# A score's PSUM bank is chosen by a rule that counts banks read by VectorE as given back four turns later

## The reference

```python
x = L0(x)   # group norm, q k v, 8 heads of 32 channels: softmax(q k^T) v, projection, + x
x = L1(x)   # group norm, + pos; three small convolutions give spatial weights; group norm;
            # 8-head attention ("1") and two single-head attentions of 128 channels ("m");
            # concatenate, silu(ff1), ff2, out_w, group norm, + residual
x = L2(x)   # group norm, q k v, 8 heads of 32 channels, projection, + normed x
x = L3(x)   # group norm, q k v, one head of 256 channels, projection, + x

def attention(q, k, v):
    weight = jax.nn.softmax(einsum("bct,bcs->bts", q, k) * scale, axis=-1)
    return einsum("bts,bcs->bct", weight, v)
```

## Time and profile before

| | us |
|---|---|
| median of three runs | 5469.68 |
| lowest and highest run | 5468.94, 5470.98 |
| the profiled execution | 5462.21 |
| its span | 5460.3 |
| TensorE busy | 4989.7 |
| VectorE, ScalarE, GpSimd busy | 2960.1, 2558.3, 3239.2 |

### The profile page before, as it was taken

How to read it: one execution, slowest core, us unless ns; L and a number is a source line. 1 busy time by engine, 2 the same in 40 slices (tenths; PEclk the granted TensorE clock), 3 DMA queues, 4 the chain that set the end, 5 groups by cost and what they waited for, 6 DMA issues and landing times.

```text
span 5460.3 us, 63207 instructions
## 1 busy us (share of the span) xinstructions
PE 4989.7 (91%) x22016; PEld 2248.6 (41%) x22016; DVE 2960.1 (54%) x5256; ACT 2558.3 (47%) x4593; POOL 3239.2 (59%) x1777
## 2 busy tenths in 40 slices
PE   7789999999999999999999998999999999999887
PEld 3235333543335433354334543345333453334434
DVE  5445666256663566526665366634666346662362
ACT  3353545435553355524555245552555525454252
POOL 4474766546674477735767357654667636675463
PEclk8889989999899999999999999999999999899988
DMA  2112111022110211102210112101212012120020
GB/s 85 29 30 59 43 46 39 20 55 54 42 30 20 72 48 33 34 22 64 54 41 19 36 50 55 47 13 44 52 45 53 7 49 61 32 53 10 14 49 12
DMA packets 103608, 221.20 MB, mean 41 GB/s; under 512 B 31104, under 2 KB 33408, under 8 KB 103168
## 3 DMA queue, kind: packets, MB, share of 16 engines
q1 hardware_dynamic: 103296, 217.16, 15.5%
HBM read 56.47 MB, written 8.39 MB: 12 GB/s over the span
## 4 chain that ended last, share of the span: by engine, by line
PE 66%; DVE 11%; issue 9%; POOL 8%; ACT 4%; SPq 1%; DMA 1%; POOLq 0%; DVEq 0%; ACTq 0%
PE bank L518 66%; DVE max_cols L953 6%; POOL probs_added L1181 4%; POOL probs_added L1168 3%; ACT probs L854 2%; DVE act L1108 1%; ACT act L864 1%; DVE dev_squared L1071 1%; DVE stats L1057 1%; POOL act L1202 1%; SPq L1268 0%; DVE sums_turned L975 0%; SPq L1257 0%; DVE sums_turned L983 0%; ACT full_parts L919 0%
## 5 line engine op out<-in xcount | busy, mean ns | idle before, releaser
L953 DVE TENSOR_REDUCE max_cols<-bank 128x1 f32<-128x512 f32 x3456 | 2187.2, 679 | 1642.0 <-PE bank L518 1638.1
L854 ACT ACTIVATE probs<-bank 128x512 f32<-128x512 f32 x3456 | 1928.9, 599 | 2378.1 <-PE bank L518 2248.9
L1181 POOL TENSOR_TENSOR probs_added<-probs_added,probs 128x1024 f32<-128x1024 f32 x768 | 1807.6, 2382 | 131.8 <-ACT probs L854 131.3
L518 PE MATMUL bank<-q_stack,k_stack 97*128 97x512 f32 (+1 forms) x3584 | 1659.9, 520 | 147.2 <-DVE max_cols L953 107.8
L518 PE MATMUL bank<-probs,v_tokens 128*32 128x512 f32 (+1 forms) x7168 | 1392.8, 645 | 41.1 <-ACT probs L854 41.1
L518 PEld LDWEIGHTS bank<-q_stack,k_stack 97*128 97x128 f32 (+1 forms) x3584 | 661.5, 195 | 880.9 <-issue 429.5
L518 PE MATMUL bank<-act,weight_stream 128*128 128x512 f32 x1792 | 941.6, 625 | 31.6 <-ACT probs L854 8.0
L1181 POOL TENSOR_TENSOR probs_added<-probs 128x1024 f32<-128x1024 f32 x192 | 452.5, 2369 | 700.2 <-PE bank L518 673.0
L1168 POOL TENSOR_TENSOR probs_added<-probs 128x512 f32<-128x512 f32 x48 | 61.0, 1270 | 885.7 <-PE bank L518 853.3
L518 PEld LDWEIGHTS bank<-probs,v_tokens 128*32 128x32 f32 (+1 forms) x7168 | 329.6, 123 | 505.6 <-issue 350.8
L518 PE MATMUL bank<-high_parts 32*128 32x512 f32 x3072 | 406.1, 516 | 108.8 <-DVE max_cols L953 59.8
(11 more groups left out here) (84 smaller groups left out, 3390.4 us busy)
## 6 DMA issues: line engine op xcount, KB each, us to landing
k_stack<-high_parts SPq DMA_DIRECT2D x384, 128.0 KB, 2.4
q_stack<-high_parts SPq DMA_DIRECT2D x768, 64.0 KB, 2.0
weight_stream<-stream_dram SPq DMA_DIRECT2D x32, 768.0 KB, 4.3
k_stack<-low_parts SPq DMA_DIRECT2D x192, 128.0 KB, 2.4
q_stack<-low_parts SPq DMA_DIRECT2D x384, 64.0 KB, 2.0
act<-x_dram SPq DMA_DIRECT2D x8, 1024.0 KB, 6.5
act<-pos_dram SPq DMA_DIRECT2D x8, 1024.0 KB, 5.9
weight_stream<-stream_dram SPq DMA_DIRECT2D x16, 512.0 KB, 3.8
```

What stands on the lines that cost most here:

```text
L518: return nc.tensor.matmul(dst, lhsT, rhs, start=start, stop=stop, **kw)
L854: act.activation(PR[:, m % P_RING, j, :], bank[:, :], ACT.Exp, scale=att.scale).then_inc(reading(key), 1)
L953: dve.tensor_reduce(cols[:, kh, j, qt:qt + 1], bank[:, :], AX.X, ALU.max).then_inc(reading(key), 1)
L1181: pool.tensor_tensor(ADD[:, js, :], one, two, ALU.add).then_inc(p_added, 1)
```

## The change

Each bank gets a flag that says whether the tile last taken in it belongs to a kind that VectorE reads (maxima, columns, sums, value results, norm means and variances, projections, ff1). When a score tile takes its bank, the `given` turn of a flagged bank counts as four turns later. For all other tiles the choice is as before. The flag is set anew at each take. The plan, the instructions and their number stay as they are; which bank a tile sits in, and so which semaphore its first matmul waits for, changes.

```diff
+BY_VECTOR = ("max", "cols", "sums", "av", "av2", "mean", "var", "proj", "ff1")
+VECTOR_LATE = 4
...
             uses, fulls, given, held = [0] * BANKS, [0] * BANKS, [0] * BANKS, {}
+            by_vector = [False] * BANKS
 
             def take(key, hold=False, says_full=True):
 
-                bank = min((i for i in range(BANKS) if i not in held.values()), key=lambda i: (given[i], i))
+
+                late = VECTOR_LATE if key[0] == "score" else 0
+                bank = min((i for i in range(BANKS) if i not in held.values()),
+                           key=lambda i: (given[i] + late * by_vector[i], i))
+                by_vector[bank] = key[0] in BY_VECTOR
                 tiles[key] = bank, uses[bank], fulls[bank]
```

## The result

| | before | changed |
|---|---|---|
| median, us | 5469.31 (4 runs) | 5567.52 (4 runs) |
| profiled execution: span, us | 5460.3 | 5560.8 |
| its mean granted clock | 0.940 | 0.930 |

The changed kernel takes 1.0182 times as long as the one before, with a 95% interval of 1.0164 to 1.0199. The forecast was 5555 us, slower, within 5420 to 5640.

The account below looks back on a forecast made before the run. In-order TensorE, busy 91% of the span, bounds the kernel by its waits and clock. 5462.21 - 76 gained + 148 lost + 19 clock = 5553 us; with the median 7.5 above, 5561, rounded to 5555; range 5420 to 5640 us.

Parts of the forecast that it names:

- the three young prices: A score on the bank of the score one, two or three ahead loses 0.87, 0.57 or 0.27 us.
- the three quarters put down: Share of the summed stall losses expected to remain, a quarter being hidden as other engines catch up.
- 148 lost less 76 gained: Stall terms: 197 us lost less 49 hidden, against gains of 14 in kind 2 and 62 ahead of other scores.
- the change's 197 us: Loss before hiding: 103, 52 and 12 us on young banks, 22 behind q tiles, 8 in kind m.
- hardly anything is lost: Kind 0, score 50: its wait moves to an exponential already awaited by the value products; nothing of 23.2 us gained.
- the 8 us that I put down as lost: Kind m, score 9: its own matmuls, 1.1 us, move behind a wait for score 7's exponential, seven times.
- 2 us each, 14 of the 25.9 us: Kind 2, score 50: it goes some 3 us earlier, the quad behind it 2 us earlier, seven times.
- the three quarters of the rest: Of the remaining 82.5 us of VectorE-caused waits ahead of scores, 62 us gained; the rest met at quads.
- The clock: TensorE's half-speed time: 49 us more from added idle time, 30 us less from spared kind 2 stretches, net 19 lost.
- The first: Rival: long stalls behind VectorE decide, not short ones behind ScalarE; faster, 5375 us; chance 0.16.
- The second: Rival: waits only change their name, gain and loss cancel; 5470 us, 5459 to 5481 called same; chance 0.08.
- the third: Rival: stalls in a row lower the clock, no kind 2 stretches go, no losses hide; 5640 us; chance 0.14.

Follow-up runs that it names:

- e1: Changed kernel, but a score never takes the bank of a score one or two matmuls back: 5485.4 us, ratio 1.0042.
- e4: Kernel before, with every fourth score of kind 2 attentions forced onto the bank of the score directly ahead: 5521.9 us, ratio 1.0110.
- e8: Changed kernel, but a score never takes the bank of the score directly ahead; two ahead stays allowed: 5499.4 us, ratio 1.0061.
- e2: Changed kernel with VectorE's banks aged by one turn instead of four: 5457.3 us, ratio 0.9987.
- e3: Changed kernel with VectorE's banks aged by eight turns instead of four: 5878.6 us, ratio 1.0766.
- e5: Kernel before, with the four turns applied only to score 50 of the kind 2 attentions: 5460.6 us, ratio 0.9987.
- e10: Kernel before, no ageing, but a score never takes the bank of a score one or two matmuls back: 5459.5 us, ratio 0.9993.
- e6: Kernel before, each tile's bank from a list: the free bank read first in the trace of before: 5365.9 us, ratio 0.9810.

## Why the prediction was right, point by point

**What bounds.** TensorE, by its waits and its clock: the other engines' busy time hardly moved with the change (VectorE by 6.3 us, ScalarE by 10.7, GpSimd by 2.5) while the span grew by 100. The mechanism, young banks behind ScalarE, is shown by e1, e4 and e8.

**The price of a stall.** 1.17 us from start to start was forecast, 1.18 and 1.25 are in the rows. That is right. What is free between two scores was put at 0.3 us and is 0.34 in the trace, which makes the three young prices some 17 of 167 us too high. In e4 less of the price was kept than the three quarters put down: 55 us, or 59 us between the profiled spans, of 142.

**Two terms of the sum were probably too large, and they lie on opposite sides.** To see them apart I took the time from each matmul's start to the next one's in each trace, and from it the shortest usual time for the same pair of forms at the clock of that moment (the lowest tenth over all kernels). What is left over is stall; what the half clock adds to the shortest time is clock. Differences to the kernel before, in us:

| kernel | span | stall | clock |
|---|---|---|---|
| changed | +100 | +69 | +32 |
| e1, both young banks barred | +12 | +22 | -9 |
| e2, one turn | -14 | -10 | -4 |
| e3, eight turns | +417 | +307 | +110 |
| e4, pairs only | +59 | +76 | -17 |
| e5, score 50 only | -8 | +2 | -10 |
| e8, next one barred | +36 | +45 | -9 |
| e10, bar alone | -13 | -1 | -11 |

The split between the last two columns depends on what is called the shortest usual time: with the median in place of the lowest tenth the change reads +61 and +41, and e4 +82 and -23.

The forecast for the change was +72 stall (148 lost less 76 gained) and +19 clock. The difference of the two terms was right, and the difference is all that is measured. The terms themselves can only be estimated. The prices of e4 add up to 142 us and gave 76 of stall, so the share kept is 0.54 and not 0.75. With it the change's 197 us become 106, and only 37 us of gain are left where I had 76. From e1 (prices 161 x 0.27 + 22 + 8 = 73 us, stall +22) the two come out smaller still, a share of 0.4 and a gain of a few us. By these two kernels the gain was between some 5 and 40 us, and the loss between 75 and 106, and the two errors cancelled: that the forecast came so near is in part luck. The share is no constant, though. In e3 the prices come to 385 us, or 415 with q tiles and kind m, and the stall is +307, a share of 0.74 at least even if nothing was gained.

**Where a part of the loss went** can be seen in kinds 0 and m. In kind 0 the value products behind score 50 wait for a norm: its coefficients on VectorE (L1083, L1091 after), the apply and the exponential on ScalarE. Before (the rest is in the earlier trace rows), and then two samples of after:

```profile
589.12 2.29 DVE L1083 TENSOR_TENSOR gn_scale<-rstd,weights 128x2 f32<-128x2 f32 x1 [1.01 <-POOL rstd L1189]
```

```profile
587.07 2.31 DVE L1091 TENSOR_TENSOR gn_scale<-rstd,weights 128x2 f32<-128x2 f32 x1 [1.04 <-POOL rstd L1197]
...
591.85 0.80 PE L521 MATMUL bank<-q_stack,k_stack 97*128 97x512 f32 x1 [3.97 <-ACT probs L862]
...
592.57 1.94 PE L521 MATMUL bank<-probs,v_tokens 128*32 128x512 f32 x8
...
2611.09 2.31 DVE L1091 TENSOR_TENSOR gn_scale<-rstd,weights 128x2 f32<-128x2 f32 x1 [1.31 <-POOL rstd L1197]
...
2615.87 0.80 PE L521 MATMUL bank<-q_stack,k_stack 97*128 97x512 f32 x1 [1.32 <-ACT probs L862]
...
2616.59 1.94 PE L521 MATMUL bank<-probs,v_tokens 128*32 128x512 f32 x8
```

The value products start 4.76 us after the coefficients before, and 5.50 us after them in the changed kernel (5.20 in two of seven samples), however early or late TensorE comes there. The stall stayed, as forecast, and became a wait for ScalarE. But "hardly anything is lost" was not quite right: the score now stands behind the wait, and its own 0.7 us are lost each time (0.4 in two of seven samples). And the stall takes up what TensorE lost earlier: before it was 3.3 us in six of seven samples, now it is 3.97 or 3.98 in two and 1.32 to 1.48 in the other five, in which TensorE comes to score 50 some 3.3 us after the coefficients instead of at their start. Over the seven samples that is some 12 us that the changed kernel lost ahead of this place and that cost nothing.

In kind m the 8 us that I put down as lost were not lost. Right behind the maximum of the earlier trace rows (by the order of takes the first behind score 9, not the second) stands another wait, which I had not read:

```profile
1774.46 0.80 PE L518 MATMUL bank<-k_stack 128*128 128x512 f32 x1 [2.09 <-ACT probs L854]
```

This maximum waits for the exponential of score 8, and it starts 4.52 us after the norm's coefficients in both kernels. The score's matmuls that moved behind the first wait (4.19 us ahead of score 9 in the changed kernel) fit into the second one.


**Why the gain was small.** The step that failed is kind 2's stall ("2 us each, 14 of the 25.9 us"), and possibly with it the three quarters of the rest. In the changed kernel the same place reads:

```profile
751.00 0.50 PE L521 MATMUL bank<-q_stack,k_stack 97*128 97x512 f32 x1 [0.33 <-ACT probs L862]
...
752.14 0.50 PE L521 MATMUL bank<-q_stack,k_stack 97*128 97x512 f32 x1 [0.65 <-ACT act L882]
...
756.03 0.80 PE L521 MATMUL bank<-high_parts 32*128 32x512 f32 x4 [2.39 <-DVE max_cols L961]
...
755.81 2.79 DVE L1116 SCALAR_TENSOR_TENSOR act<-act 32x512 f32<-32x512 f32 x3
...
758.63 0.69 DVE L961 TENSOR_REDUCE max_cols<-bank 128x1 f32<-128x512 f32 x1
...
759.47 1.88 PE L521 MATMUL bank<-act,weights 96*32 96x512 f32 x2 [1.91 <-DVE max_cols L961]
```

Score 49 and the convolution in the timeline of before:

```profile
747.36 0.49 PE L518 MATMUL bank<-q_stack,k_stack 97*128 97x512 f32 x1 [0.34 <-ACT probs L854]
...
756.43 1.92 PE L518 MATMUL bank<-act,weights 96*32 96x512 f32 x2
```

The quad came earlier, as forecast: 5.03 us after the start of score 49 (751.00) instead of 6.78 (754.14 less 747.36), 1.75 us against my 2. What I had not done is read on. Score 51 was the next to wait for a maximum before, 0.76 us; now it doesn't, and the convolution behind it has got that maximum's bank. VectorE comes to this maximum only behind L1116 (L1108 before) and is done with it at 758.63 + 0.69 = 759.32. The convolution started 8.47 us after score 49 here and 9.07 before, so 0.60 us of the 1.75 are left; in e5, where score 51 waits for its maximum besides, it is 9.09 (754.38 less 745.29), and nothing is left. e5's ratio leaves 7 us of the 44 that I had put down there, clock and all.

**The quads.** I forecast their wait to stay near 109 us; it fell to 73.4, nearly all in the part that ScalarE causes. That fits: a score that has waited for an exponential leaves the quad less to wait for.

**The clock** was undersized, 19 against 32 us (41 by the other split). The mechanism, short stalls in a row, is seen at a place where the kernel before ran at full clock from 815 to 860 us. Stretches of before, then of after (columns as in the earlier trace rows):

```profile
815.00:860.00 45.00, 43.65 (x239) 18.71 (x231) 27.47 (x48) 27.44 (x52) 36.48 (x18) 1.00 0.17 41
```

```profile
827.00:836.00 9.00, 7.80 (x56) 2.32 (x48) 5.44 (x10) 4.14 (x9) 3.51 (x2) 1.00 0.34 82
836.00:846.00 10.00, 9.74 (x31) 2.89 (x31) 4.50 (x8) 3.31 (x6) 8.14 (x4) 0.50 0.01 2
...
863.00:870.00 7.00, 7.00 (x27) 2.60 (x30) 2.48 (x4) 3.19 (x7) 1.91 (x2) 0.53 0.37 83
```

The two matmul rows of after just ahead of the fall:

```profile
834.73 0.73 PE L521 MATMUL bank<-q_stack,k_stack 97*128 97x512 f32 x2 [0.69 <-ACT probs L862]
835.98 0.77 PE L521 MATMUL bank<-q_stack,k_stack 97*128 97x512 f32 x1 [0.51 <-ACT probs L862]
```

Stalls of 0.69 and 0.51 us, both on young banks, stand ahead of ten microseconds at half speed. The prediction had let the trace support what it names from the Trainium skill ("TensorE: Matmul & The Clock Gate", "A second HAM failure mode: psum-queue depth-cycling") for long stalls only; here it agrees for short ones. Even the trace of before has such falls, which the prediction had missed:

```profile
1553.48 0.50 PE L518 MATMUL bank<-q_stack,k_stack 97*128 97x512 f32 x1 [0.28 <-DVE max_cols L953]
```

```profile
1554.80:1568.40 13.60, 13.45 (x52) 4.48 (x44) 8.44 (x17) 7.06 (x13) 3.63 (x3) 0.50 0.12 29
```

Counted over the whole traces, 22 of 84 falls before, and 46 of 106 in the changed kernel, have no idle time of 1 us or more in the 8 us ahead (a choice of this count, not something the chip was seen to do). The half-speed time that starts so is 109 us before and 296 in the changed kernel, of 658 and 784 us in all. So the new half-speed time stands behind short stalls. But it isn't a rule of so much clock per stall: e4 has as much more stall as the change, 76 against 69 us, and its clock's part fell by 17. Which clusters of stalls bring the clock down stays open. The difference between kernels with nearly equal stalls (e5, e10, before: -10, -11, 0 us of clock) is scatter: over all its runs e5 has a mean clock of 0.942 and e10 of 0.942, and the kernel before beside them 0.941 and 0.942, while the profiled execution of e10 is the fastest of its twelve. So some 10 us of the clock column should not be read.

**The rivals.** The first (VectorE's long stalls decide) falls by e1 and e5. The second (the waits change their name) is right for single places, kind 0, kind m and kind 2's score 50, and wrong for the whole, by e6. Of the third, the larger loss, only the clock's part came near (49 us put down, 32 or 41 found); some of the losses did hide.

## What to carry to other kernels

When one in-order engine writes buffers that several readers give back, the bank that comes free next is set by when its reader gets to it, not by which engine reads it: count how many takes fall on a buffer filled one or two instructions ago before preferring one reader's buffers, since such a take costs the full round trip (here 1.2 us from start to start instead of 0.34). A long wait that is set by another chain, as kind 0's norm, takes up what was lost ahead of it, so the same small stall costs less in front of such a place. A wait behind a reader that is itself behind is not removed by taking another buffer; the next tile that needs that reader pays it, so read the timeline past the first tile that moves. A choice made from the read times of a trace (1.9% here) shows that more is to be had than such a rule brings, though not how much at most, and a small preference with a bar on the youngest buffers (0.6%) is a rule that keeps part of it.

## What was not expected of the hardware

Two stalls of 0.69 and 0.51 us, 1.25 us from start to start, were followed by 10 us at half of TensorE's clock, at a place where the kernel before ran at the full clock. A kernel with as much stall spread in another way ran at a slightly higher mean clock than the kernel before: 0.942 to 0.946 in the four runs of e4, against 0.937 to 0.944 in the 19 runs beside it. And one and the same stall of 3.7 us was followed by 17 us at half speed in some samples and by 44 us in others.
